# GpSimd's sum of two accumulators issued ahead of its add of key tile 8

## What is computed

```python
def _attn(x, Wq, bq, Wk, bk, Wv, bv, Wo, bo):
    B, L, _ = x.shape                        # 2, 2048
    def heads(y):
        return y.reshape(B, L, H, HD).transpose(0, 2, 1, 3)   # H 16, HD 32
    q = heads(x @ Wq + bq)
    k = heads(x @ Wk + bk)
    v = heads(x @ Wv + bv)
    scores = jnp.einsum('bhqd,bhkd->bhqk', q, k) / np.sqrt(HD).astype(x.dtype)
    attn = jax.nn.softmax(scores, axis=-1)
    out = jnp.einsum('bhqk,bhkd->bhqd', attn, v)
    out = out.transpose(0, 2, 1, 3).reshape(B, L, D)
    return out @ Wo + bo
```

## Time and profile before

| | us |
|---|---|
| median of 3 runs | 3049.31 (3049.03 to 3049.62) |
| the profiled execution | 3049.14 |
| its span in the profile | 3047.8 |
| granted TensorE clock, mean | 0.997 |
| share of the span: PE, DVE, POOL, ACT | 98%, 70%, 52%, 45% |

### The profile page before, as it was taken

How to read it: one execution, slowest core, us unless ns; L and a number is a source line. 1 busy time by engine, 2 the same in 40 slices (tenths; PEclk the granted TensorE clock), 3 DMA queues, 4 the chain that set the end, 5 groups by cost and what they waited for, 6 DMA issues and landing times.

```text
span 3047.8 us, 42422 instructions
## 1 busy us (share of the span) xinstructions
PE 2993.2 (98%) x15850; PEld 2089.7 (69%) x15850; DVE 2144.6 (70%) x3627; ACT 1385.1 (45%) x2673; POOL 1579.5 (52%) x685
## 2 busy tenths in 40 slices
PE   7999999999999999999999999999999999999999
PEld 6887655555555555555555546788888888789998
DVE  5558889899998989999899988643333333235666
ACT  3221577666666666666667663321111111022332
POOL 0000489899998999999899994400000000102222
PEclk9999999999999999999999999999999999999999
DMA  7683798989999899898998977720111110311221
GB/s 236 204 250 125 174 196 192 200 187 204 206 196 203 186 201 206 193 209 190 200 206 190 202 168 226 244 85 1 42 42 42 42 42 16 111 65 63 86 81 67
DMA packets 174013, 455.32 MB, mean 149 GB/s; under 512 B 19045, under 2 KB 61157, under 8 KB 142672
## 3 DMA queue, kind: packets, MB, share of 16 engines
q0 software_dynamic: 32064, 232.54, 37.3%
q1 hardware_dynamic: 139938, 214.51, 23.0%
q10 hardware_dynamic: 1806, 5.56, 0.7%
HBM read 143.47 MB, written 75.50 MB: 72 GB/s over the span
## 4 chain that ended last, share of the span: by engine, by line
PE 64%; POOL 15%; DMA 14%; DVE 3%; issue 3%; ACT 2%; SPq 0%; POOLq 0%; DVEq 0%; ACTq 0%
DMA pt<-pt 12%; PE ps L1296 11%; PE ps L1283 11%; POOL pt L949 9%; PE ps L427 7%; PE ps L742 6%; PE ps L753 6%; PE ps L525 5%; PE ps L1851 4%; POOL pt L921 3%; PE ps L529 3%; PE ps L1868 3%; ACT pt L837 2%; PE ps L1888 1%; DMA x<-in_x 1%
## 5 line engine op out<-in xcount | busy, mean ns | idle before, releaser
L440 DVE TENSOR_REDUCE nmp<-ps 128x1 f32<-128x512 f32 x1966 | 1200.6, 681 | 58.8 <-PE ps L427 56.7
L837 ACT ACTIVATE pt<-ps 128x512 f32<-128x512 f32 x2048 | 1030.9, 629 | 447.9 <-PE ps L742 426.5
L949 POOL TENSOR_TENSOR pt<-pt 128x2048 f32<-128x2048 f32 x217 | 1099.4, 5066 | 11.1 <-ACT pt L837 6.4
L742 PE MATMUL ps<-qs,ks 128*128 128x512 f32 x2048 | 803.1, 396 | 5.0 <-ACT pt L837 4.9
L427 PE MATMUL ps<-ks,qs 128*128 128x512 f32 x1966 | 802.3, 408 | 0.1
L427 PEld LDWEIGHTS ps<-ks,qs 128*128 128x128 f32 x1966 | 368.8, 188 | 264.8 <-DVE nmp L440 172.6
L753 PE MATMUL ps<-pt,vq 128*32 128x512 f32 x4096 | 492.5, 598 | 0.0
L742 PEld LDWEIGHTS ps<-qs,ks 128*128 128x128 f32 x2048 | 383.6, 188 | 114.6 <-ACT pt L837 34.1
L1283 PE MATMUL ps<-hpb,w 128*128 128x512 f32 x1536 | 376.9, 395 | 0.0
L1296 PE MATMUL ps<-w,gp 128*128 128x512 f32 x1536 | 369.3, 389 | 3.0 <-DVE gp L1412 3.0
L1296 PEld LDWEIGHTS ps<-w,gp 128*128 128x128 f32 x1536 | 288.1, 188 | 64.1 <-DVE gp L1412 4.3
(11 more groups left out here) (180 smaller groups left out, 2801.0 us busy)
## 6 DMA issues: line engine op xcount, KB each, us to landing
pt<-pt POOLq DMA_DIRECT2D x219, 1024.0 KB, 9.7
qk_d<-st SPq DMA_DIRECT2D x128, 256.0 KB, 2.9
qs<-qk_d SPq DMA_DIRECT2D x87, 256.0 KB
ks<-qk_d SPq DMA_DIRECT2D x42, 512.0 KB, 5.7
xina<-in_x SPq DMA_DIRECT2D x8, 1024.0 KB, 6.7
v_d<-vst SPq DMA_DIRECT2D x32, 256.0 KB, 2.6
vq<-v_d SPq DMA_DIRECT2D x32, 256.0 KB, 8.2
ao_d<-accs SPq DMA_DIRECT2D x32, 256.0 KB, 3.2
```

What stands on the lines that cost most here:

```text
L440: dve.tensor_reduce(nmp[:, n // 4, n % 4:n % 4 + 1], ps[:, ring.bank["max", u], :], AX.X, ALU.max, negate=True).then_inc(s_mr, 1)
L742: pe.matmul(ps[:, score_bank(n), :], ksb[w % 2][:, hh, 128 * kt:128 * kt + 128], qsb[:, v % 3, hh, :], start=True, stop=True).then_inc(s_s ...
L837: act.activation(pt[:, exp_slot(g), hh, :], ps[:, score_bank(n), :], ACT.Exp, scale=SCALE).then_inc(s_exp, 1)
L949: pool.tensor_tensor(accumulator(v, 0), accumulator(v, 0), pt[:, exp_slot(g), :, :], ALU.add).then_inc(s_add, 1)
```

## The change

In the units 1 to 30, the merge of the preceding unit moves on GpSimd. Before, it stood behind add 8 and DMA 9, ahead of `pool_values`. Now it stands behind DMA 7 and ahead of add 8.

```diff
@@ -940,6 +940,8 @@
                             pool.wait_ge(s_dma[d], dma_count(v, d, kt) - 16)
                         pool.dma_start(accumulator(v, 1 + d), pt[:, exp_slot(g), :, :],
                                        accum_op=ALU.add).then_inc(s_dma[d], 16)
+                if 0 < v < NU - 1 and kt == 8:
+                    pool_merge(v - 1)
                 if v < NU - 1 and kt in ADD_POOL:
                     pool.wait_ge(s_exp, 4 * g + 4)
                     if kt == ADD_POOL[0]:
@@ -950,8 +952,6 @@
                                        ALU.add).then_inc(s_add, 1)
                 if v == NU - 2 and kt == 15:
                     pool_merge(v)
-                if 0 < v < NU - 1 and kt == 9:
-                    pool_merge(v - 1)
                 if kt == (5 if v == NU - 1 else 9) and v >= 2:
                     pool_values(v - 2)
                 if kt == 10 and v == NU - 1:
```

## The result

The changed kernel takes 3061.47 us (median of 4 runs, 3060.06 to 3069.12), and the kernel before 3049.47 beside it (4 runs, 3049.03 to 3049.9). The ratio is 1.0044, with an interval of 1.0027 to 1.0062. The forecast was 3047.6, with a range up to 3058; the time lies 3.5 us outside it, on the slower side. The profiled execution took 3062.09 us, its span 3060.8, which is 13.0 more than before.

A forecast was written before the change was run, and what follows sets the result against it. GpSimd's closed loop over DMA 3 was taken to set the pace. From 3049.14 us profiled, 0 for the merge, 0 for add 8 and DMA 9 and -1.5 for covered waits gave 3047.6, range 3041 to 3058.

The follow-up runs named there:

- e6: On the kernel before, DMA 3 issued ahead of the fold at key tile 3, the fold given a semaphore of its own: 3035.07 us, ratio 0.9957.
- e2: On the kernel before, the two DMAs of the next unit's row maxima issued ahead of the output store on SyncE's queue: 3050.68 us, ratio 1.0002.

## What to carry to other kernels

When a large DMA is moved in time, looking at who waits for it is half of the work: list every transfer, of every queue, that is issued within its length at the new place, and ask who waits for those. A copy of 8 KB that a matmul waits for is worth as much care as a megabyte. When an edit moves a transfer by a count on a semaphore, measure in the trace by how much it moved: the same two counts were 0.9 us in one direction and 3.0 in the other. And where the pace is a closed loop, open the loop first (here two issues swapped, e6): an edit that costs 17 us inside the loop gained 6 once it was open.

## What was not expected of the hardware

- A 1 MB accumulating DMA of GpSimd's queue held small DMAs of SyncE's queue for as long as it lasted: 128 packets against none in 5 us, rows of 8 KB landing after 4.8 us instead of 2.3, a store of 256 KB after 5.5 instead of 3.2 (medians). With the rows issued ahead of the store and 0.27 us behind DMA 9, in the kernel before, they took 5.2 us as well (e2).
- The query and key loads cost nothing when they went 0.9 us earlier and 53 us when they went 3.0 us later; in the second case DMA 3 took 16.2 us on the mean instead of 13.8.
- An accumulating DMA of 1 MB took 13.8 us on the mean as DMA 3 behind the fold, and 9.5 when it went ahead of it; the fold then took 14.1 instead of 9.3. In both orders the one issued second was the slow one.
